# A megakernel of two layers: tokens reach the experts by products with tables of ones, and nine places for expert weights instead of thirteen

## The reference, cut to what matters

```python
E, K, H, I, CAP = 64, 8, 256, 96, 64
logits = x @ gate_w.T                       # x: 1024 x 256
probs = softmax(logits)
w, sel = top_k(probs, K)
w = w / sum(w)
pos = (how many earlier choices fell on the same expert)
valid = pos < CAP
xin = zeros((E, CAP + 1, H)).at[eid, slot].set(x[tok])    # rows to their places
inp = xin[:, :CAP]
h = silu(inp @ wg) * (inp @ wu)             # per expert 64x256 @ 256x96
out = h @ wd                                # per expert 64x96 @ 96x256
y = sum over the 8 choices of w * valid * out[eid, slot]
```

## Time and profile before

| | |
|---|---|
| median of 3 runs | 723.96 us (717.58 to 724.84) |
| profiled execution, its own time | 719.88 us |
| its span, first to last instruction | 718.1 us |
| mean granted TensorE clock, as a share of 2.4 GHz | 0.894 |
| busy, share of the span | PE 78%, PEld 59%, DVE 62%, ACT 43%, POOL 36% |
| chain that ended last, by engine | PE 44%, DVE 24%, issue 10%, DMA 7%, POOL 5%, ACT 4%, unknown 3%, SP queue 2% |
| moved by DMA | 62.90 MB |

### The profile page before, as it was taken

How to read it: one execution, slowest core, us unless ns; L and a number is a source line. 1 busy time by engine, 2 the same in 40 slices (tenths; PEclk the granted TensorE clock), 3 DMA queues, 4 the chain that set the end, 5 groups by cost and what they waited for, 6 DMA issues and landing times.

```text
span 718.1 us, 9581 instructions
## 1 busy us (share of the span) xinstructions
PE 563.4 (78%) x3092; PEld 423.2 (59%) x3092; DVE 444.9 (62%) x981; ACT 307.5 (43%) x951; POOL 260.4 (36%) x305
## 2 busy tenths in 40 slices
PE   2996998596506657476377999999999799998996
PEld 0553676374304434345254777677677688887885
DVE  5729466352398436331688799999786565745444
ACT  2664445242203423232257887887886211111110
POOL 2225507635573311116664554631110355610000
PEclk9899999786557967789687999999999999999999
DMA  8700135331305999882222232330000000000000
GB/s 309 306 1 0 38 128 199 110 104 54 93 0 148 283 310 303 265 306 81 74 58 53 31 50 40 49 41 1 1 1 1 1 0 1 1 8 22 1 1 29
DMA packets 28753, 62.90 MB, mean 88 GB/s; under 512 B 7779, under 2 KB 11025, under 8 KB 28192
## 3 DMA queue, kind: packets, MB, share of 16 engines
q1 hardware_dynamic: 20000, 41.30, 18.3%
q0 software_dynamic: 8704, 21.00, 11.5%
HBM read 48.63 MB, written 17.83 MB: 93 GB/s over the span
## 4 chain that ended last, share of the span: by engine, by line
PE 44%; DVE 24%; issue 10%; DMA 7%; POOL 5%; ACT 4%; another core or an unknown queue 3%; SPq 2%; POOLq 0%; DVEq 0%; ACTq 0%
PE bank L1269 40%; DMA arena<-in_usc 3%; POOL expert_in L392 2%; DVE arena L1099 2%; ACT arena L748 2%; DMA arena<-in_dsc 2%; DVE arena L1195 2%; POOL arena L422 1%; POOL arena L427 1%; SPq L313 1%; DMA arena<-in_wmod 1%; DVE arena L1164 1%; DVE arena L934 1%; DMA expert_out<-arena 1%
## 5 line engine op out<-in xcount | busy, mean ns | idle before, releaser
L1269 PE MATMUL bank<-arena 128*128 128x128 f32 (+9 forms) x1848 | 366.9, 389 | 38.0 <-DMA arena<-in_wmod 8.3
L1269 PEld LDWEIGHTS bank<-arena 128*128 128x128 f32 (+4 forms) x1848 | 249.9, 188 | 122.4 <-issue 76.1
L392 POOL DMA_INDIRECT expert_in<-arena x64 | 65.5, 1024 | 67.3 <-DVE arena L996 46.6
L855 ACT ACTIVATE arena<-bank 128x512 f32<-128x512 f32 x32 | 19.2, 599 | 113.4 <-PE bank L1269 113.4
L1250 DVE TENSOR_TENSOR arena<-arena,bank 128x512 f32<-128x512 f32 x32 | 22.0, 687 | 56.6 <-ACT arena L855 56.6
L1269 PE MATMUL bank<-h_hi,gu_hi 128*128 128x512 f32 x128 | 50.7, 396 | 1.0 <-issue 0.5
L1269 PE MATMUL bank<-h_low,gu_hi 128*128 128x512 f32 x128 | 50.5, 394 | 0.0
L1269 PE MATMUL bank<-h_hi,low 128*128 128x512 f32 x128 | 50.1, 391 | 0.0
L456 POOL TENSOR_TENSOR low<-arena,gu_hi 128x128 fp32r<-128x128 f32 x64 | 29.9, 499 | 55.4 <-DVE dn_hi L1199 55.4
L422 POOL DMA_INDIRECT arena<-expert_out,arena x32 | 37.1, 1160 | 9.2 <-issue 8.4
L1269 PE MATMUL bank<-dn_hi,it_hi 128*128 128x256 f32 x128 | 36.4, 285 | 3.9 <-DVE it_low L1252 3.9
(11 more groups left out here) (235 smaller groups left out, 1040.5 us busy)
## 6 DMA issues: line engine op xcount, KB each, us to landing
arena<-in_wgu SPq DMA_DIRECT2D x32, 384.0 KB, 4.8
arena<-in_wd SPq DMA_DIRECT2D x32, 192.0 KB, 6.7
expert_in<-arena SPq DMA_DIRECT2D x1, 4096.0 KB, 23.8
arena<-expert_in POOLq DMA_DIRECT2D x16, 256.0 KB, 7.1
expert_out<-arena POOLq DMA_DIRECT2D x16, 256.0 KB, 7.1
arena<-in_w SPq DMA_DIRECT2D x1, 2048.0 KB, 9.1
arena<-in_wmod SPq DMA_DIRECT2D x1, 1536.0 KB, 15.3
arena<-in_w_in SPq DMA_DIRECT2D x1, 1288.0 KB, 8.9
```

The lines of the kernel that those rows point to most:

```text
L392: pool.indirect_dma_start(xin, bass.IndirectOffsetOnAxis(scatter8[:, t, k:k + 1], 0), h[:, t, :], None, bounds_check=SLOTS - 1, oob_is_err ...
L855: act.activation(gl[n % 3], bank[2 * (n % 3)][:, :], ACT.Gelu_apprx_tanh).then_inc(gl_ready, 1)
L1269: return pe.matmul(o, lhsT, rhs, start=start, stop=stop, **kw)
```

## The change

- `expert_in`, its zero fill, the 64 scatters, the loads of rows and the buffers `xg` are gone.
- GpSimd splits the normalized rows of each tile in two f32r parts: `h_hi`, and what is left, in place of `h`. That is two instructions of 128x256 a tile.
- For each group VectorE makes a table `spot` of ones and zeros, 128 x 8 tiles x 256 places: four comparisons (one an expert) of a token's negative position (`negpos`) with the number of the place (`minus_c`). Two tables are held.
- `rows_T(g)` becomes 32 products: for both halves of the 256 values and all 8 tiles, `h_hi` and the rest (128x128, stationary) times `spot` (128x256, moving), added up in PSUM. This puts the rows in place and transposes them at once. It waits for the table of g instead of a load.
- VectorE's order: two tables ahead of the loop; in round g `hid(g)`, table g+2, in round 0 also all of `w8`, then the decodes. Before, `w8` stood ahead of the loop, and one chunk of decodes too (NEARLY 1 becomes 0).
- Places for expert weights: NS = 9 instead of 13, since the tables and the parts need room.
- The attention weights wait for `down_mm` 14 and all of `xgT_mm` (the count of finished `rows_T`) instead of `down_mm` 13.

```diff
-        NS = 13
+        NS = 9
...
-        NX = 4
-        xg = [at(XB + 5120 + 512 * i, 2, DM) for i in range(2)] + [at(XB + 512 * i, 2, DM) for i in range(2)]
+        h_hi = [at((A1 + 360, XB + 5120)[t // 4] + DM * (t % 4), DM) for t in range(T)]
+        spot = [at(A0 + 7168 + 2048 * i, T, 2 * P) for i in range(2)]
+        negpos = at(XB, T, E)
...
-        NEARLY, PACE = 1, 1.5
+        NEARLY, PACE = 0, 1.5
...
-            sp.wait_ge(zero_set, 1)
-            sp.dma_start(xin.rearrange("(p r a) c -> p r (a c)", p=P, r=8), under(zero, 8)).then_inc(xin_zeroed, 16)
...
-            for q, tile, early in ((0, 1, True), (1, 2, True), (2, 2, True), (3, 3, True), (6, 3, True), (12, 4, True), (4, 1, False),
-                                   (5, 2, False), (7, 4, False), (8, 5, False), (9, 6, False), (10, 7, False)):
+            for q, tile, early in ((0, 1, True), (1, 2, True), (2, 2, True), (3, 3, True), (6, 3, True), (4, 1, False),
+                                   (5, 2, False), (7, 4, False), (8, 5, False)):
                 sp.wait_ge(st_mm if early else yT_mm, tile)
                 load_pair(q)
             sp.wait_ge(yT_mm, T)
-            load_pair(11)
...
-                    sp.wait_ge(down_mm, 13)
+                    sp.wait_ge(down_mm, 14)
+                    sp.wait_ge(xgT_mm, NG)
                     sp.dma_start(w12_s, w1).then_inc(ld_c_w12, 16)
...
-            pool.wait_ge(xin_zeroed, 16)
             for t in range(T):
-                pool.wait_ge(slots_ready, t + 1)
-                for k in range(TOPK):
-                    pool.indirect_dma_start(xin, bass.IndirectOffsetOnAxis(scatter8[:, t, k:k + 1], 0), h[:, t, :], None,
-                                            bounds_check=SLOTS - 1, oob_is_err=False).then_inc(scattered, 16)
+                pool.wait_ge(rowsT_mm, T + t + 1)
+                if t >= 4:
+                    pool.wait_ge(st_mm, 4)
+                pool.tensor_copy(rounded(h_hi[t]), h[:, t, :]).then_inc(pool_chain, 1)
+                pool.wait_ge(pool_chain, T + t + 1)
+                pool.tensor_tensor(rounded(h[:, t, :]), h[:, t, :], rounded(h_hi[t]), ALU.subtract).then_inc(halves_ready, 1)
...
-                link(dve.max(slot8[:, t, :], slotv[:, t, :]))
-                dve.tensor_scalar(scatter8[:, t, :], slot8[:, t, :], -1.0, NOWHERE, ALU.mult, ALU.add).then_inc(slots_ready, 1)
+                link(dve.tensor_tensor(negpos[:, t, :], slotv[:, t, :], rows_s[:, 24:88], ALU.subtract))
+                dve.max(slot8[:, t, :], slotv[:, t, :])
...
+            def spots(g):
+                if g >= 2:
+                    dve.wait_ge(xgT_mm, g - 1)
+                for i in range(4):
+                    ins = dve.tensor_tensor(rounded(spot[g % 2][:, :, CAP * i:CAP * (i + 1)]), over(negpos[:, :, 4 * g + i], CAP),
+                                            under(minus_c, T), ALU.is_equal)
+                ins.then_inc(spot_ready, 1)
+
+            dve.wait_ge(yT_mm, T)
+            spots(0)
+            spots(1)
+
+            def expert_weights():
...
                 dve.tensor_tensor(hid[g % 2], sg[g % 2], up, ALU.mult).then_inc(hid_ready, 1)
+                if g + 2 < NG:
+                    spots(g + 2)
+                if g == 0:
+                    expert_weights()
                 while late < 2 * NQ and late < 2 * NEARLY + (g + 1) * PACE:
                     decode(late // 2, late % 2)
...
             def rows_T(g):
-                pe.wait_ge(xg_loaded[g % NX], 16 * (g // NX + 1))
+                pe.wait_ge(spot_ready, g + 1)
                 if g >= 2:
                     pe.wait_ge(xgT_ready, 2 * (g - 1))
-                for q in range(2):
-                    for j in range(KC):
-                        ins = pe.transpose(bank[g % 2][:, (2 * q + j) * P:(2 * q + j + 1) * P], xg[g % NX][:, q, j * P:(j + 1) * P], ident)
+                for j in range(KC):
+                    for t in range(T):
+                        for part in (h_hi[t], h[:, t, :]):
+                            ins = mm(bank[g % 2][:, 2 * P * j:2 * P * (j + 1)], rounded(part[:, j * P:(j + 1) * P]), rounded(spot[g % 2][:, t, :]),
+                                     start=t == 0 and part is h_hi[t], stop=t == T - 1 and part is not h_hi[t])
                 ins.then_inc(xgT_mm, 1)
```

More of the change, by code:

```diff
@@ L174, in adaln_two_layers @@
             sem, ["h2_ready", "logits_mm", "lmax_ready", "exp_ready"])
-        mask_ready, pos_mm, place_read, slots_ready, scattered = map(
-            sem, ["mask_ready", "pos_mm", "place_read", "slots_ready", "scattered"])
+        mask_ready, pos_mm, place_read, halves_ready, spot_ready = map(
+            sem, ["mask_ready", "pos_mm", "place_read", "halves_ready", "spot_ready"])
         wout_ready, cols_mm = sem("wout_ready"), sem("cols_mm")
         w_loaded = [sem(f"w_loaded{i}") for i in range(NS)]
-        xg_loaded = [sem(f"xg_loaded{i}") for i in range(NX)]
         xgT_mm, xgT_ready, gu_mm, sg_ready, hid_ready, hidT_mm, hidT_ready, down_mm, ob_ready = map(
@@ L247, in adaln_two_layers @@
         X1 = X0 + 2048
-        places = [(A0 + 2048 * i, "gu_hi") for i in range(4)] + [(A0 + 8192, None)] + [(B0 + 2048 * i, "low") for i in range(6)] + [
-            (D0, None), (D0 + 1536, "it_low"), (D0 + 3072, "it_hi"), (D0 + 4608, None), (A1, "h4_hi"), (A1 + 1024, None),
+        places = [(2048, "h"), (4096, None)] + [(A0 + 2048 * i, "gu_hi") for i in range(4)] + [
+            (A0 + 7168, "spot"), (A0 + 9216, "spot"), (A0 + 11264, None)] + [(B0 + 2048 * i, "low") for i in range(6)] + [
+            (D0, None), (D0 + 1536, "it_low"), (D0 + 3072, "it_hi"), (D0 + 4608, None), (A1, "h4_hi"),
             (X0, "dn_hi"), (X1, "h4_low"), (X1 + 1088, "h4_low"), (X0 + 4224, "dn_hi"), (X0 + 6272, None), (X0 + 8448, "h4_hi"),
-            (X0 + 9472, None)]
+            (X0 + 9472, None), (X0 + 10240, "h_hi")]
         split = []
-        gap = ctx.enter_context(nc.sbuf_tensor("gap", [P, A0], f32))
+        gap = ctx.enter_context(nc.sbuf_tensor("gap", [P, places[0][0]], f32))
         for n, (start, name) in enumerate(places):
@@ L385, in _, with store_rows @@
                 pool.tensor_tensor(x[:, t, :], x[:, t, :], h[:, t, :], ALU.add).then_inc(xh_ready, 1)
-            pool.wait_ge(xin_zeroed, 16)
             for t in range(T):
-                pool.wait_ge(slots_ready, t + 1)
-                for k in range(TOPK):
-                    pool.indirect_dma_start(xin, bass.IndirectOffsetOnAxis(scatter8[:, t, k:k + 1], 0), h[:, t, :], None,
-                                            bounds_check=SLOTS - 1, oob_is_err=False).then_inc(scattered, 16)
[L395 to L407, removed]
+                pool.wait_ge(rowsT_mm, T + t + 1)
[4 more added lines that the diff above has]
+                pool.tensor_tensor(rounded(h[:, t, :]), h[:, t, :], rounded(h_hi[t]), ALU.subtract).then_inc(halves_ready, 1)
+            def store_rows(g):
                 pool.wait_ge(ob_ready, g + 1)
@@ L410, in _ @@
                     .then_inc(ob_stored[g % 3], 16)
+            for g in range(NG):
+                store_rows(g)
             for i in range(3):
@@ L582, in copy_rows @@
                     act.wait_ge(gu_mm, g - 1)
[L583 removed]
+                by_chunk = xgT[g % 2].rearrange("p (q j) c -> p j q c", j=KC)
                 for j in range(KC):
[L585 removed]
+                    act.activation(by_chunk[:, j], bank[g % 2][:, 2 * P * j:2 * P * (j + 1)].rearrange("p (q c) -> p q c", q=2), ACT.Identity,
                                    scale=h2_cols[:, KC + j:KC + j + 1], bias=h2_cols[:, j:j + 1]).then_inc(xgT_ready, 1)
@@ L1043, in _ @@
[L1043 to L1050, removed]
-            ins.then_inc(w8_ready, 1)
+            def spots(g):
[5 more added lines that the diff above has]
+                ins.then_inc(spot_ready, 1)
@@ new lines, in _ @@
+            dve.wait_ge(yT_mm, T)
+            spots(0)
+            spots(1)
+            def expert_weights():
+                link(dve.tensor_tensor(eqk, prob, mask_b, ALU.mult))
+                link(dve.tensor_reduce(rsum, eqk, AX, ALU.add))
+                dve.reciprocal(rsum, rsum)
+                link(dve.tensor_tensor(wvalid, wvalid, prob, ALU.mult))
+                link(dve.tensor_tensor(wvalid, wvalid, over(rsum, E), ALU.mult))
+                link(dve.tensor_scalar(eqk[:, :, 0:TOPK], slot8, -1.0, NOWHERE, ALU.mult, ALU.add))
+                link(dve.tensor_scalar(gather8, eqk[:, :, 0:TOPK], float(SLOTS - 1), None, ALU.min))
+                for k in range(TOPK):
+                    link(dve.tensor_tensor(eqk, slotv, over(slot8[:, :, k], E), ALU.is_equal))
+                    link(dve.tensor_tensor(eqk, eqk, wvalid, ALU.mult))
+                    ins = dve.tensor_reduce(w8[:, :, k], eqk, AX, ALU.add)
+                    if k < TOPK - 1:
+                        link(ins)
+                ins.then_inc(w8_ready, 1)
```

14 lines of the change are left out of this document (3 added, 11 removed).

## The result

| | before | after |
|---|---|---|
| median of the runs, us | 724.21 | 765.18 |
| fastest to slowest, us | 717.58 to 724.84 | 762.08 to 767.32 |
| profiled execution: its span, us | 718.1 | 765.5 |

The ratio is 1.060 with a 95% interval of 1.054 to 1.065: slower by 41 us, or 5.4 to 6.5%. The forecast was 765. The profiled execution of the kernel after took 767.32 us, 2 over its median, and that of the kernel before 719.88, 4 under its own, so between the two profiles the difference is 47 us and not 41.

What follows compares the result with a forecast made beforehand. It took the expert stage as bound by transfers, with unnamed pieces in the state-space loop. 719.9 + 51.5 (later stage end) + 13 (clock) - 21.9 (pieces) = 762.5, raised to 765 towards the median; range 742 to 793.

Steps and rivals of the forecast that it cites:

- the pieces: State-space loop: five chain pieces with no named releaser, taken to go with the scatters, -21.9 us; bounds 0 and -21.9.
- the delay behind the last place: Expert stage, from the last place to the last `copy_out`: later end, +51.5 us, and clock loss, +13.
- The closed loop: Expert rounds: VectorE's comparisons stand behind `hid`, so nothing runs ahead and the period is the sum, 9.1 us.
- the comparisons: VectorE's four comparisons making each group's table in the expert loop: 2.7 us, bounds 2.4 and 2.9.
- `gate_up` to silu: Expert loop: from the start of `gate_up` until ACT starts its silu, 1.57 us of the period.
- The clock: Expert loop: TensorE's granted clock at 0.85, +1.0 us for each of 13 rounds, +13; bounds 0 and +73.
- `w8` bare: Group 0 of the expert stage: VectorE's expert-weight arithmetic, 20.9 us, no longer under the scatters and nearly all bare.
- Nothing for nine places, the zero fill, GpSimd's split and the attention weights: Loads hide with nine places; zero fill at the start 0; GpSimd's split of h 0; attention weights +1 at most.
- Rival 1: State-space loop: the unnamed pieces stay, being TensorE's own matter, 787 us; chance 0.25.
- Rival 3: Expert loop stays at the full clock and the comparisons overlap, 748 us; chance 0.10.
- Rival 4: Expert loop does not close, comparisons and row products run ahead of `hid`, 708 us, faster than before; chance 0.04.
- Rival 2: Expert loop: clock at 1.2 GHz, at half the rounds 36 us instead of 13, 788; chance 0.08.

Runs made afterwards that it cites:

- e_order: Kernel after, with the comparisons of group g+2 moved ahead of hid(g) on VectorE's queue; 718.49 us, ratio 0.998 to the kernel before.
- e_half_products: Kernel after, without the 16 row products a group that take the low part of h; 736.58 us, ratio 1.024 to the kernel before.
- e_half_spots: Kernel after, with two of the four comparisons of each group from group 2 on; 729.98 us, ratio 1.012 to the kernel before.
- e_filler: Kernel after, with 14 unused products added behind the last product of each of 13 rounds; 749.08 us, ratio 1.035 to the kernel before.
- e_both: Kernel after, with comparisons moved ahead of hid(g) and the eight places of `w8` spread over rounds 1 to 8; 713.53 us, ratio 0.991 to before.
- e_w8_spread: Kernel after, with the eight places of `w8` spread over rounds 1 to 8 and the gate's chunks unpacked last; 751.46 us, ratio 1.046 to before.
- e_scatter_late: Kernel before, with all 64 scatters held until the places of all eight tiles are there; 767.26 us, one run.
- e_after_scatters: Kernel after, with the 64 scatters put back in the state-space loop, into memory that nothing reads; 786.32 us, ratio 1.087 to the kernel before.
- e_ns9_before: Kernel before, with nine places for expert weights, first loads in the after order, attention weights behind `down_mm` 14; 724.43 us, ratio 0.999 to before.

## Why the prediction was right

- **The time and the sign.** 765 was forecast and 765.2 measured. By its terms: the pieces -21.9, measured -22.9 by the last place; the delay behind the last place, 51.5 + 13 = 64.5, measured 185.6 against 117.6 from the last place to the end of the last `copy_out`, 67.9. Both are off a little, in opposite directions: +45.0 for the end of the stage against 42.6. That the sum meets the median to within 0.2 us is luck. The sum starts from a profiled execution 4 us under its median and came to 762.5, 4.8 short of the profiled execution after, which itself lies 2 over its median; with the 2 us put on top these differences cancel. The five pieces add up to 21.84, which the prediction has as 21.9, and the last place moves by some 2 us either way from kernel to kernel: in the eight others that have no scatters in the loop, its MAX8 starts between 176.3 and 180.2.
- **The closed loop** was the step on which all rested, and it is shown by e_order, e_half_products and e_half_spots. Its size at the full clock, 9.1 us, is near what e_filler has: 8.99. Of the terms, `rows_T` was 3.84 and takes 32 x 0.12; the comparisons were 2.7 and take 2.49; `gate_up` to silu was 1.57 and takes 238.58 - 237.01 = 1.57.
- **The clock** was +1.0 us a round and +13 in all. The size was too small. From the first row product to the last it is 5.29 us in the mean of twelve rounds (231.45 to 347.12) against 3.78 in e_filler: 1.5 us a round, 18 us in e_filler's time. A round was 10.1 by the prediction and is 10.5 in the mean (218.13 to 354.84). The mechanism was also put too loosely. It is not a steady loss but a stretch of some 3 us at 1.2 GHz (in one round 6 us) within each round's row products. With waits of 0.49 to 0.56 us (e_filler) and 1.16 to 1.22 (e_half_spots) in the same place no such stretch came in twelve rounds each, so the wait matters. What decides in between was not found: in e_both a wait of 1.84 us had the stretch and one of 1.86 did not, and in e_w8_spread one of 2.36 us (before 278.75) had none.
- **`w8` bare**: forecast 41.9 us from the last place to `hid(1)`, measured 218.13 - 176.75 = 41.4. That it was bare is shown in the trace of e_w8_spread, which takes 16.8 us from that gap, and its time confirms 10 us of it (4 to 15).
- **The unnamed pieces**: at 0 or -21.9, I took -21.9, and e_scatter_late and e_after_scatters show that they come and go with the scatters in the loop. The reading that TensorE had issued its products and only its counts came late does not hold for all of it: in the longest piece TensorE has no product on record from 131.81 to 135.39. The rule of the Trainium skill (SBUF — State Buffer, section "Who interferes with whom"), that a DMA never contends with a compute engine, would have put the sum at 787. Here the last place came 21.5 us later with the scatters in the loop than without in the kernel before (199.40 against 177.89), and 25.3 in the kernel after (202.06 against 176.75). Whether that goes by way of a port or by another no run here tells.
- **Nothing for nine places, the zero fill, GpSimd's split and the attention weights**: e_ns9_before shows the first and part of the last. GpSimd's last subtraction took 0.72 us, as the product of the earlier trace rows does, and ended at 172.9, before the comparisons began:

```profile
172.21 0.72 POOL L389 TENSOR_TENSOR h<-arena,h_hi 128x256 fp32r<-128x256 f32 x1
```

From the end of the last `copy_out` to the end of the span the two kernels differ by 47.4 - 45.0 = 2.4 us. The prediction allowed 1 for the attention weights at most and put nothing in its sum.
- **The rivals.** Rival 1 (the pieces stay, being TensorE's own matter, 787) is refuted by the last place at 176.75. e_after_scatters, which brings pieces back, comes to 786, but some 5 us of its 20 go with the late split. Rival 3 (full clock, 748) did not come by itself; e_filler, which makes the full clock, took 749. Rival 4 (an open loop, 708) is e_order: 718.5, since it has `w8` whole in one round, 27.2 us from `hid(0)` to `hid(1)`. The point from which it decides was put at 6.6 us a group; e_order has 6.53 and comes out level with before. Rival 2 (1.2 GHz through half of the rounds, +36) did not come: the clock took 18 us, between the forecast's 13 and this rival's 36.

## What to carry to other kernels

When a transfer is replaced by arithmetic, write down for each engine the order of its queue over one round, and follow the dependences until they close. Here the new work (2.5 us of comparisons) fitted easily into VectorE's idle time, but it stood one call too late in its queue, so that a round was the sum of its members instead of the longest. Moving the call made 44 us, more than the comparisons themselves, because the wait for them had also cost clock. And look at what the removed wait had been hiding: `w8` was free under the scatters, cost up to 21 us in the open, and was free again under the gathers. With both moves the change is worth 4% instead of costing 6%.

## What the runs showed of the hardware

- A short wait cost more than its length. TensorE waited 2.36 to 2.42 us in each of twelve rounds of some 10 us, and in each of them a stretch of the row products behind the wait ran at 1.2 GHz, 1.5 us more a round; filling the wait with 14 products that nothing reads gave 18 us in all. The stretch began with or just behind the first product in seven of the rounds and further in in the other five (at 295.94, 1.3 us behind the start at 294.65). Not every wait of that length had it, as said above.
- f32r products of 128x256 with a fresh weight tile each follow each other by 0.118 us at 2.4 GHz and by 0.213 us at 1.2 GHz. Four comparisons with 512 results each and two broadcast inputs take 2.49 us when they are not chained, so they start 0.60 us apart; the chained instructions of the same size in `w8` start 0.72 us apart (204.02 to 204.75 before) and take 0.69.
- While GpSimd issued indirect scatters in the state-space loop, the engines stood for stretches whose releaser no row names, in the longest one TensorE, ScalarE and VectorE for 3.58, 5.94 and 8.74 us. This came in both kernels and went with the scatters: the last place was 21 to 25 us later with them.
